# A one-hot of 128 rows instead of 16 in the bias products of a routed mixture of experts

## The reference, cut to what matters

```python
def swiglu(x, w1, b1, w2, b2, w3, b3):          # for each of E = 8 experts; D = 256, H = 512
    p1 = x @ w1 + b1                            # 256 -> 512
    p2 = x @ w2 + b2
    return (silu(p1) * p2) @ w3 + b3            # 512 -> 256
scores = softmax(x @ gate_w + gate_b)
weights, indices = top_k(scores, 2)             # two experts for each token
routed = sum over the two of weights * swiglu of that expert
out = x + mean over 2 shared experts + routed
```

## Time and profile before

| | |
|---|---|
| median of 3 runs | 2931.27 us (2926.65 to 2938.2) |
| span of the profiled execution | 2925.5 us (its time outside the span is not listed) |
| mean granted TensorE clock | 0.875 of full speed |
| PE busy | 2332.4 us, 80% of the span |
| PEld busy | 1412.3 us, 48% |
| DVE busy | 1681.5 us, 57% |
| ACT busy | 1018.2 us, 35% |
| POOL busy | 357.1 us, 12% |

### The profile page before, as it was taken

The page is one execution under the profiler, slowest core; times in us unless marked ns, Lnnn a source line. Parts: engine busy times, 40 slices in busy tenths (PEclk is TensorE's granted clock), DMA queues, the critical chain, the costliest instruction groups (busy, mean ns, idle before and its releaser), DMA issues. The chain is left out here.

```text
span 2925.5 us, 49732 instructions
## 1 busy us (share of the span) xinstructions
PE 2332.4 (80%) x17258; PEld 1412.3 (48%) x17259; DVE 1681.5 (57%) x2614; ACT 1018.2 (35%) x1925; POOL 357.1 (12%) x431
## 2 busy tenths in 40 slices
PE   3898888753698999999799669899999999945051
PEld 2666666552584555555487553333333333315041
DVE  4776777541242333333266338789888988747842
ACT  2444444211230000000022223667677777731010
POOL 2000000016200000000134420000000000020034
PEclk9999999656799999999999886899999999975576
DMA  6000000135512111111232589454546453021034
GB/s 202 2 0 0 0 0 0 51 125 191 187 43 87 33 35 36 33 35 36 86 101 86 201 236 82 37 50 38 48 36 53 37 48 27 2 67 52 0 115 144
DMA packets 218149, 193.26 MB, mean 66 GB/s; under 512 B 117482, under 2 KB 193938, under 8 KB 215986
## 3 DMA queue, kind: packets, MB, share of 16 engines
q1 hardware_dynamic: 203058, 140.34, 24.8%
q0 software_dynamic: 12672, 34.62, 3.8%
q10 hardware_dynamic: 2304, 16.78, 1.6%
HBM read 109.62 MB, written 81.79 MB: 65 GB/s over the span
## 5 line engine op out<-in xcount | busy, mean ns | idle before, releaser
L1650 DVE TENSOR_REDUCE ga_nmax<-banks 128x1 fp32r<-128x1024 f32 x512 | 621.3, 1221 | 122.6 <-PE banks L1721 121.0
L1680 ACT ACTIVATE ga_probT<-banks 128x512 f32<-128x512 f32 x1024 | 553.8, 597 | 251.6 <-PE banks L1734 207.9
L1721 PE MATMUL banks<-a_ks,a_qs 48*128 48x512 f32 x1024 | 397.8, 476 | 65.3 <-DVE ga_nmax L1650 19.9
L1734 PE MATMUL banks<-a_qs,a_ks 49*128 49x512 f32 x1024 | 392.8, 465 | 7.8 <-DMA a_qs<-ga_max_rows 7.1
L1750 PE MATMUL banks<-ga_probT,a_v 128*32 128x256 f32 (+1 forms) x3840 | 334.6, 422 | 6.2 <-ACT ga_o L1686 6.2
L1721 PEld LDWEIGHTS banks<-a_ks,a_qs 48*128 48x128 f32 x1024 | 166.3, 201 | 289.0 <-DVE ga_nmax L1650 164.3
L1183 PE MATMUL banks<-m_w,rb_xT 128*128 x576 | 288.8, 624 | 0.0
L1030 PE MATMUL banks<-sh_xnT,sh_w 128*128 128x512 f32 x768 | 188.7, 403 | 45.7 <-DVE sh_w L943 23.7
L1165 ACT ACTIVATE rb_silu<-banks 128x512 f32<-128x512 f32 x72 | 43.0, 597 | 516.2 <-PE banks L1183 516.2
L1030 PEld LDWEIGHTS banks<-sh_xnT,sh_w 128*128 128x128 f32 x768 | 148.3, 195 | 82.4 <-issue 52.3
L1734 PEld LDWEIGHTS banks<-a_qs,a_ks 49*128 49x128 f32 x1024 | 161.4, 195 | 29.5 <-ACT ga_probT L1680 19.0
(11 more groups left out here) (288 smaller groups left out, 3479.2 us busy)
## 6 DMA issues: line engine op xcount, KB each, us to landing
sh_xnT<-xnT_parts ACTq DMA_DIRECT2D x16, 1024.0 KB, 4.9
sorted_rows<-wa_zero SPq DMA_DIRECT2D x1, 9216.0 KB, 28.9
rb_xb<-sorted_rows POOLq DMA_DIRECT2D x72, 128.0 KB, 2.3
sorted_out<-rb_yb SPq DMA_DIRECT2D x72, 128.0 KB, 1.7
xnT_parts<-np_parts SPq DMA_DIRECT2D x8, 1024.0 KB, 4.5
m_w<-in_L_ffn_rw_dram SPq DMA_DIRECT2D x2, 4096.0 KB
values<-pg_v SPq DMA_DIRECT2D x16, 512.0 KB, 2.7
a_v<-values SPq DMA_DIRECT2D x16, 512.0 KB, 11.2
```

Source lines behind the costliest of these rows:

```text
L1650: nc.vector.tensor_reduce(nmax[b % 2][:, at:at + 1], slot[:], axis=AX.X, op=ALU.max, negate=True).then_inc(use_read, 1)
L1680: nc.scalar.activation(probT[k % SETS][2 * h + n][:], b_t[w % RING][:], ACT.Exp, scale=SCALE).then_inc(exp_ready, 1)
L1721: return nc.tensor.matmul(slot[:, HALF * kh:HALF * (kh + 1)], qs[a][rows, n, P * q:P * (q + 1)], ks[a][rows, n, HALF * kh:HALF * (kh + 1)] ...
L1734: nc.tensor.matmul(b_t[w % RING][:], ks[a][rows, 2 * gp + n, P * kt:P * (kt + 1)], qs[a][rows, 2 * gp + n, HALF * hf:HALF * (hf + 1)], sta ...
```

## The change

`b_parts`, `row_e`, `row_at`, `own` and `own_out` get 128 partitions instead of 16. GpSimd clears `b_parts` first; VectorE waits for that and then writes the 16 rows that hold biases. The comparison now runs in all 128 partitions; in rows 16 to 127 `row_e` is 8 to 119, which is no expert's number, so the one-hot is 0 there and multiplies rows of zeros. What is computed stays the same.

```diff
-        b_parts = sb("b_parts", [2 * E, 2 * H + D], F32R)
+        b_parts = sb("b_parts", [P, 2 * H + D], F32R)
         rest = sb("rest", [2 * E, 1])
-        row_e, row_at = sb("row_e", [2 * E, P]), sb("row_at", [2 * E, P])
-        own = [sb(f"own{s}", [2 * E, P], F32R) for s in range(2)]
-        own_out = sb("own_out", [2 * E, P], F32R)
+        row_e, row_at = sb("row_e", [P, P]), sb("row_at", [P, P])
+        own = [sb(f"own{s}", [P, P], F32R) for s in range(2)]
+        own_out = sb("own_out", [P, P], F32R)
...
             nc.gpsimd.iota(rest[:], pattern=[[0, 1]], base=0, channel_multiplier=1, **io)
+            nc.gpsimd.memset(b_parts[:].bitcast(F32), 0.0).then_inc(b_zero, 1)
             nc.gpsimd.iota(row_at[:], pattern=[[0, P]], base=0, channel_multiplier=1, **io).then_inc(rest_set, 1)
...
-            link(nc.vector.scalar_tensor_tensor(b_parts[:], b_hi[:].bitcast(F32), rest[:, 0:1], b_all[:], ALU.mult, ALU.add))
+            dve.wait_ge(b_zero, ONE + 1)
+            link(nc.vector.scalar_tensor_tensor(b_parts[0:2 * E], b_hi[:].bitcast(F32), rest[:, 0:1], b_all[:], ALU.mult, ALU.add))
...
-                nc.vector.tensor_scalar(own[s][:], row_e[:], block_f[0:2 * E, bass.ds(j, 1)], None, ALU.is_equal).then_inc(own_ready, 1)
+                nc.vector.tensor_scalar(own[s][:], row_e[:], block_f[:, bass.ds(j, 1)], None, ALU.is_equal).then_inc(own_ready, 1)
...
-                nc.vector.tensor_scalar(own_out[:], row_e[:], block_f[0:2 * E, bass.ds(j, 1)], None, ALU.is_equal)
+                nc.vector.tensor_scalar(own_out[:], row_e[:], block_f[:, bass.ds(j, 1)], None, ALU.is_equal)
```

More of the change, by code:

```diff
@@ L1069, in routed_blocks @@
         yb = [sb(f"yb{s}", [P, D]) for s in range(2)]
-        w_in, b_in, step, rest_set = sem("w_in"), sem("b_in"), sem("step"), sem("rest_set")
+        w_in, b_in, step, rest_set, b_zero = sem("w_in"), sem("b_in"), sem("step"), sem("rest_set"), sem("b_zero")
         xb_in, kept = g.pool_dma(2), [sem(f"kept{s}") for s in range(2)]
```

## The result

| | before | after |
|---|---|---|
| median of 4 runs | 2928.96 us (2924.62 to 2938.2) | 2849.12 us (2835.37 to 2859.06) |
| span of the profiled execution | 2925.5 us | 2847.7 us (its own time 2849.31) |
| PE busy | 2332.4 us | 2255.6 us |
| DVE busy | 1681.5 us | 1683.8 us |
| POOL busy | 357.1 us | 358.6 us |

The ratio of after to before is 0.9727, with a 95% interval of 0.9692 to 0.9763: faster, by about 80 us. The forecast was 2847 us, counted from the median of three runs before (2931.3); a fourth run brought that median to 2928.96.

A forecast was written before the change was run, and what follows sets the result against it. TensorE's own stream was taken to bound the routed blocks, with gaps around each 16-row bias product. Removing them gains 84 us: the span goes from 2925.5 to 2841.5, the median from 2931.3 to 2847 us, range 2838 to 2892 us.

The forecast's parts named there:

- The bound: Routed blocks: nothing but TensorE's own stream sets the time; it is busy 524.00 of 524.00 us.
- Rival D: Routed blocks: `own` or `gluT` come late by 0.2 to 0.3 us a step, giving 2865 us; chance 0.03.
- 0.39 us of gaps for a bias product: Routed blocks: three bias products a step lose 0.39 us each, 1.18 us of a 7.563 us step.
- The three parts: Around a bias product: 0.09 us late ahead, 0.195 us more in it, a bare load of 0.105 us behind.
- One sign: Routed blocks' trace: a single load behind each bias product in place of the pair would show the forecast right.
- 84 us: Gain in the routed blocks: 72 x 1.18 = 85.0 us, less 0.8 and 0.1 that were hidden.
- Height and not type: Bias products: the 0.39 us gaps come from 16 rows among full-height products, not from fp32r among float32.
- rival B: Behind each bias product: the return to float32 keeps its gap, 42 us stay, giving 2889 us; chance 0.11.
- Rival C: Bias products' loads: they can't be hidden, or height is not what decides; nothing happens, 2931 us; chance 0.08.
- rival E: TensorE in the routed blocks: a denser stream lowers the clock; half the stage there gives 3077 us; chance 0.03.
- The comparisons: `own` and `own_out` on VectorE: each grows by 0 to 0.14 us, taken as 0; even 0.14 fits the slack.
- The memset: Start of the routed blocks, GpSimd: 1.2 us, delays the first two blocks' loads, hidden behind VectorE's work on `b_parts`.

The follow-up runs named there:

- e6: The changed kernel without its 216 bias products, leaving the routed experts' biases out of the result: 2814.77 us, ratio 0.9605 to the kernel before.
- e1: The change made with padded tensors of 64 rows instead of 128: 2937.78 us, ratio 0.9997 to the kernel before.
- e5: The change made with padded tensors of 72 rows instead of 128: 2843.9 us, ratio 0.9713 to the kernel before.
- e4: The kernel before, with each 16-row bias product issued twice in a row: 2970.17 us, ratio 1.0112 to the kernel before.
- e7: The changed kernel with the shared experts' and the gate's bias products also padded to 128 rows: 2838.77 us, ratio 0.9687 to the kernel before.

## Why the prediction was right

- **The bound.** TensorE's stream alone sets the routed blocks' time. Right: its busy share is 100% of the long stretch in both traces, and nothing new waits. `own` ends at 1004.38, its load starts at 1005.19: 0.8 us of slack, as worked out. `gluT` ends at 1002.57, L1210's load starts at 1003.45: 0.9, as worked out. Rival D had nothing to stand on.
- **0.39 us of gaps for a bias product, step 6.39 us.** Right: 6.40 measured. The three parts (ahead, in it, behind) were read from distances of starts, and all three are gone. e6 shows that what remains is the stream. One sign was worded too simply: not a single load stands behind the bias product but still two in one row, in 0.42 us instead of 0.30; the first starts while the product streams, the second with the first L1185 record.
- **84 us.** The stage fell by 83.0. The program's median fell by 80, and the four runs after scatter by 24 us; that it ends within 2 us of the forecast is in part luck.
- **Height and not type.** Right, and now shown directly: the type changes in the same places, and the gaps are gone (e6); they come back with 64 rows (e1). What I called "equal height" was too strict, though: 72 rows beside 128 are as good as 128 (e5), and 64 as bad as 16. My next guess, the quarters in use, fell with e5.
- **The return to float32** (rival B, 2889 us) had no row of its own; L1042 and L526 pointed the right way, and e6 settled it: a step of 6.40 us with the products and 5.82 without leaves 0.58 for them, and B needed 0.59 more.
- **Rival C**, with the Trainium skill's rule that a weight load overlaps a running matmul only in other row groups (TensorE: Matmul & The Clock Gate, Part 3, "The mechanism"), would have left the time at 2931. The measurement decides: loads of all rows overlap matmuls of all rows, here L1185's at 1001.39. The opening of the same section also lets a load run ahead when it targets the background weight buffer, which I left out of the prediction. What stops the overlap in this kernel is that 16 or 64 rows meet 128 (steps of 7.56 and 7.57 us); 16 beside 16 does not (e4).
- **The clock** (rival E) stayed at 1.00 in the stretch.
- **The comparisons** grew by 0.01 us each (0.27 to 0.28), not by 0.14. **The memset** delayed the first blocks' loads as forecast, and was hidden as forecast. The kernel after, start of the stage, against the earlier trace rows:

```profile
883.38 1.16 POOL L1098 MEMSET rb_b_parts<- 128x1280 f32 x1
...
884.69 1.17 POOL L1102 DMA_DIRECT2D rb_xb<-sorted_rows  x2
...
887.59 0.69 PE L1178 MATMUL banks<-ident,rb_xb 128*128 128x128 f32 x2 [6.13 <-DMA rb_xb<-sorted_rows]
...
889.38 0.42 DVE L1126 COPY rb_xT<-banks 128x256 f32<-128x256 f32 x1
```

1.16 us for the memset (1.2 estimated), transposes 1.2 us later (887.59 against 886.38), and the copy that follows VectorE's work on `b_parts` not later at all (889.38 against 889.77).

## What to carry to other kernels

Where a product with few contraction rows stands alone among full ones, look at the starts of the weight loads around it. A load that starts with the matmul ahead of its own is hidden; one that comes later (here 0.20 us after the last transpose) is not, and a busy share of 100% conceals it. Compare with the matmul ahead and not with its own: the hidden load at 1001.28 also stands only 0.03 us before its own record. Here each such stretch cost 0.39 us, and padding its operands with zero rows to 72, 112 or 128 removed all of it. The padding cost nothing on TensorE: three products of 128 rows take 0.58 us a step (e6), three of 16 rows next to others of 16 take 0.60 (e4). If padding isn't possible, putting low products next to each other may help: in e4 the price was per stretch, not per product.

## What the runs showed of the hardware

- Between products of 128 rows, one of 72 or 112 rows behaves like one of 128 (steps of 6.41 and 6.41 us, and 6.40), one of 16 or 64 does not (7.56 and 7.57 us). I had expected the boundary at the quarters of the array.
- A change from float32 to fp32r and back costs nothing at full height (0.58 us for three products whose streams are 0.57). The records only start at unusual distances: the fp32r record comes 0.03 us after the last transpose (1001.28 to 1001.31), the next float32 record 0.31 after that, and the sum, 0.34, is that of the two streams (0.11 and 0.227).
- The runs of one kernel scatter by ±0.4%, which hides a change of a few us, and a part of it sits in the second layer's attention, which no kernel here changed. It took about 834 us before, 839 after, 820 in e4 and 843 in e7, in step with the clock granted there (the number behind POOL's count). The stretches of before, after, e4 and e7:

```profile
1755.00:2589.00 834.00, 770.81 (x6208) 303.66 (x6208) 670.04 (x671) 575.97 (x1089) 0.17 (x2) 0.92 0.48 40
```

```profile
1673.00:2512.00 839.00, 777.95 (x6206) 305.28 (x6207) 670.11 (x670) 575.92 (x1089) 0.19 (x2) 0.91 0.46 40
```

```profile
1797.00:2617.00 820.00, 758.72 (x6208) 298.83 (x6206) 669.75 (x671) 575.37 (x1089) 0.00 (x0) 0.94 0.48 41
```

```profile
1659.00:2502.00 843.00, 785.90 (x6208) 308.65 (x6206) 670.72 (x671) 575.43 (x1089) 0.00 (x0) 0.90 0.47 40
```

The same matmuls (6206 to 6208 recorded), the same work on VectorE and ScalarE within 1 us, and 23 us between the clocks 0.94 and 0.90. Why the clock differs from run to run there stays open.
